# A gated attention and mixture-of-experts kernel: softmax denominators by on-chip transfers, reciprocals at step 11, and a reordered SyncE queue

## The reference, cut to what matters

```python
x = x + tanh(g_xattn) * cross_attention(layernorm(x), ctx)     # 8 heads, 512 queries, 512 keys
x = x + tanh(g_ffn) * moe(layernorm(x))                        # 8 experts, the best 2, and a shared one
# inside cross_attention, per batch and head
attn = softmax(q @ k.T / sqrt(16));  out = attn @ v
```

## Time and profile before

| what | value |
|---|---|
| runs, median (lowest to highest) | 1438.15 us (1435.48 to 1442.34) |
| the profiled execution | 1441.5 us, its span 1439.6 us |
| mean granted TensorE clock | 0.974 of full speed |
| TensorE, VectorE, ScalarE, GpSimd busy | 93%, 68%, 61%, 60% of the span |

### The profile page before, as it was taken

One profiled execution on the slowest core, in us unless ns is written; L12 is line 12 of the kernel. 1 busy time (PEld: TensorE's weight loads), 2 busy tenths in 40 slices (PEclk: granted clock), 3 DMA queues, 4 the chain that ended last, 5 costly groups with the idle time before them and its releaser, 6 DMA issues.

```text
span 1439.6 us, 24599 instructions
## 1 busy us (share of the span) xinstructions
PE 1339.7 (93%) x7290; PEld 648.5 (45%) x7290; DVE 974.5 (68%) x1661; ACT 872.5 (61%) x1720; POOL 867.6 (60%) x1278
## 2 busy tenths in 40 slices
PE   2899999999999989998989999989999999999997
PEld 1222222222222222232222222267778888888886
DVE  5888788988788878897878888656654333333332
ACT  2588787877777767786767777734333433333332
POOL 7447667767776777677767864633212555555553
PEclk7799999999999999999999999999999999999999
DMA  6566666666767666766666766276653788785655
GB/s 177 160 190 206 191 202 198 195 199 185 188 178 181 197 183 174 187 199 181 180 182 185 188 160 172 92 206 138 150 183 82 188 215 205 182 198 110 111 110 81
DMA packets 161308, 247.90 MB, mean 172 GB/s; under 512 B 33605, under 2 KB 58828, under 8 KB 161182
## 3 DMA queue, kind: packets, MB, share of 16 engines
q1 hardware_dynamic: 142926, 208.96, 51.6%
q0 software_dynamic: 18256, 37.38, 14.0%
HBM read 141.85 MB, written 103.88 MB: 171 GB/s over the span
## 4 chain that ended last, share of the span: by engine, by line
PE 34%; DMA 21%; SPq 12%; issue 11%; DVE 9%; POOL 8%; ACT 4%; POOLq 1%; ACTq 0%; DVEq 0%
PE m_banks L949 17%; DMA parts_k<-arena 11%; SPq L470 8%; DMA arena<-pv_d 6%; DVE row_max L1122 6%; PE bank L906 4%; PE bank L877 4%; PE m_banks L856 3%; PE bank L837 3%; SPq L456 3%; POOL xs L780 2%; DMA out<-xs,ids 2%; POOL arena L679 2%; POOL arena L676 2%; POOL arena L677 2%
## 5 line engine op out<-in xcount | busy, mean ns | idle before, releaser
L1122 DVE TENSOR_REDUCE row_max<-m_banks 128x2 f32<-128x1024 f32 x512 | 614.4, 1220 | 82.1 <-PE m_banks L856 77.5
L1394 ACT ACTIVATE arena<-bank 128x512 f32<-128x512 f32 x1024 | 556.6, 606 | 127.8 <-PE bank L877 124.8
L877 PE MATMUL bank<-arena 112*128 112x512 bf16 x1024 | 317.7, 389 | 6.0 <-ACT arena L1394 1.8
L906 PE MATMUL bank<-arena 128*32 128x512 f32 x2048 | 278.9, 617 | 0.3 <-ACT arena L1401 0.3
L792 POOL DMA_INDIRECT out<-xs,ids x71 | 112.5, 1584 | 173.6 <-ACT xs L1468 138.4
L856 PE MATMUL m_banks<-arena 48*128 48x512 bf16 x1024 | 169.7, 395 | 27.0 <-DVE row_max L1122 20.7
L877 PEld LDWEIGHTS bank<-arena 112*128 112x128 bf16 x1024 | 79.7, 100 | 255.5 <-ACT arena L1394 91.6
L949 PE MATMUL m_banks<-w_ring,h_hi 128*128 x568 | 183.1, 403 | 0.0
L1457 ACT ACTIVATE arena<-m_banks 128x256 f32<-128x256 f32 x103 | 39.5, 384 | 190.4 <-PE m_banks L949 190.3
L676 POOL TENSOR_TENSOR arena<-arena 128x512 bf16<-128x512 f32 x62 | 71.6, 1156 | 110.3 <-ACT arena L1386 107.4
L856 PEld LDWEIGHTS m_banks<-arena 48*128 48x128 bf16 x1024 | 39.7, 94 | 164.1 <-issue 81.9
(11 more groups left out here) (176 smaller groups left out, 2037.9 us busy)
## 6 DMA issues: line engine op xcount, KB each, us to landing
pv_d<-arena SPq DMA_DIRECT2D x32, 512.0 KB, 4.3
w_ring<-split_d SPq DMA_DIRECT2D x60, 256.0 KB
parts_k<-arena SPq DMA_DIRECT2D x96, 128.0 KB
parts_q<-arena SPq DMA_DIRECT2D x96, 128.0 KB
arena<-parts_k SPq DMA_DIRECT2D x64, 192.0 KB, 3.7
arena<-parts_q SPq DMA_DIRECT2D x64, 192.0 KB, 3.8
arena<-in_w SPq DMA_DIRECT2D x36, 256.0 KB, 7.0
arena<-in_ctx SPq DMA_DIRECT2D x32, 256.0 KB, 3.4
```

Source lines behind the costliest of these rows:

```text
L877: nc.tensor.matmul(out, k_stack[b % 3][0:SHIFTED, h, kt * P:(kt + 1) * P], q_stack[b % 3][0:SHIFTED, h, :], start=True, stop=True).then_in ...
L906: last = nc.tensor.matmul(pv_ps[2 * DH * j:2 * DH * (j + 1), :], v_ones[b % 3][:, kt, GROUP * g + j, :], probs[pair % 3][:, j, :], start=( ...
L1122: nc.vector.reduce_max(pair, m_ps[(STEPS * b + u) // 2 % M_PAIRS], AX_X).then_inc(s_mx, 1)
L1394: nc.scalar.activation(probs[group % 3][:, j, :], bank_of["scores", b, s], ACT.Exp, scale=float(DH) ** -0.5).then_inc(s_exp, 1)
```

## The change

Instead of reading the denominators back from memory, SyncE copies them inside SBUF, with one transfer per half g: 4 partitions of 512 words become 64 partitions of 32. It needs only that `take_values` has written both halves. These two transfers stand ahead of `store_values`. The reciprocals are taken at step 11 instead of 16. `store_reciprocals` moves ahead of `load_ctx` and `store_turned`. The next batch's row of maxima, `row(i + 1, 0)`, moves ahead of the query reads `read(i + 2, 1)`. `load_values` now waits for the landing of `store_values` itself, and `take_values` waits for the previous batch's on-chip transfers.

```diff
-RECIP_AT = 16
+RECIP_AT = 11
-            def load_denominators(b):
-                sp.wait_ge(s_w, DMA * (b + 1))
+            def spread_denominators(b):
+                sp.wait_ge(s_u, 2 * b + 2)
                 if b:
                     sp.wait_ge(s_rc, b)
-                sp.dma_start(den_c, pv_d[:, DH, :].rearrange("h (c w) -> h c w", c=DH)).then_inc(s_sc, DMA)
+                for g in range(2):
+                    sp.dma_start(den_c[P // 2 * g:P // 2 * (g + 1), :], pv_sb[DH:P:2 * DH, g, :]).then_inc(s_sc, DMA)
...
             def load_values(b):
                 sp.wait_ge(s_r, DMA * (b + 1))
+                sp.wait_ge(s_w, DMA * (b + 1))
...
                 if is_b(i - 1):
+                    spread_denominators(i - 1)
                     store_values(i - 1)
...
                 if is_b(i - 1):
-                    load_denominators(i - 1)
+                    store_reciprocals(i - 1)
                 if is_b(i + 4) and i + 4 >= 2:
                     load_ctx(i + 4)
                 if is_b(i - 3):
                     store_turned(i - 3)
-                if is_b(i - 1):
-                    store_reciprocals(i - 1)
+                if is_b(i + 1):
+                    row(i + 1, 0)
                 if is_b(i + 2):
                     read(i + 2, 1)
-                if is_b(i + 1):
-                    row(i + 1, 0)
...
                 if j == 0:
+                    spread_denominators(B - 1)
                     store_values(B - 1)
                 if j == 1:
                     store_turned(B - 3)
-                    load_denominators(B - 1)
...
             def invert(b):
-                dve.wait_ge(s_sc, DMA * (b + 1))
+                dve.wait_ge(s_sc, 2 * DMA * (b + 1))
...
                 if b:
                     act_e.wait_ge(s_w, DMA * b)
+                    act_e.wait_ge(s_sc, 2 * DMA * b)
                 nc.scalar.copy(pv_sb[:, g, :], pv_ps).then_inc(s_u, 1)
```

## The result

The changed kernel takes 1420.87 us in the median of 17 runs (1412.53 to 1432.76), against 1441.42 us for the kernel before, measured beside it (17 runs, 1435.48 to 1450.13). The ratio is 0.9856 [0.9833, 0.988]: 20.6 us gained, where 39.7 were forecast. The profiled execution took 1418.35 us, with a span of 1416.5.

What follows compares the result with a forecast made beforehand. The reciprocal's wait for denominators, queued on SyncE behind the reads of k, was taken as the bound. 42 - 4 + 1.7 = 39.7 us gained gave 1399 us against the median; range 1390 to 1411, chance 0.78.

Steps and rivals of the forecast that it cites:

- The 42 us: Reciprocal's wait at step 16 goes, each of 28 turns falling from 28.02 to 26.5 us; 42 gained, bounds nothing to 47.
- the wait that comes at step 11: Reciprocals moved to step 11 wait for late on-chip transfers; 4 us lost, range 1 to 29.
- The landings: On-chip transfers at step 11, measured by `row`: 2.8 us median, 6.0 worst; backlog 0.8 us later costs 6.7, 2 us 29.
- The price of a wait: At step 11: the first 0.9 us free in a turn, each us beyond costs about 1.2.
- Rival A: Wait moves from step 16 to 11, transfers landing 2 us or more later; 29 us lost, 1411 to 1425, chance 0.15.
- Rival B: Query reads behind the row come late, TensorE waits each turn; 81 us against 42 gained, 1477, chance 0.03.
- cost 0, 1.7 us to spare: Row of maxima ahead of query reads: last read landed at 22.6, wanted at 24.3 in a 26.5 us turn; cost 0.
- The last batch: End of the attention: `source(2)` goes out about 4 us earlier without the wait for the store; 1.7 us gained.
- The signs named in advance: Profile after: reciprocal's wait under 12 us, TensorE idle near 20, turns of 26.5 throughout, SyncE longest at row of maxima.

Runs made afterwards that it cites:

- number 1: The kernel after with the reciprocals back at step 16 instead of 11: 1401.81 us, 0.9742.
- number 2: The kernel after with the query reads ahead of the row of maxima again, reciprocals still at step 11: 1411.65 us, 0.9795.
- 3  on-chip, old order: The kernel before with the on-chip transfers alone: reciprocals at step 16, old order of store_reciprocals and query reads: 1411.62 us, 0.9799.
- 4  row first alone: The kernel before with only the row of maxima moved ahead of the query reads, denominators still read back from memory: 1493.21 us, 1.0366.
- number 5: The kernel after with load_values ahead of the row of maxima, reciprocals at step 11: 1434.84 us, 0.9959.
- 6  step 13: The kernel after with the reciprocals at step 13 instead of 11: 1409.78 us, 0.9789.
- 8  on-chip ahead of row: The kernel after with the two on-chip transfers ahead of row(i, 1) instead of behind it: 1417.56 us, 0.9842.
- 9  reads first, step 13: The kernel after with the query reads ahead of the row of maxima and the reciprocals at step 13: 1411.81 us, 0.9815.
- number 12: The kernel after with the two on-chip transfers issued by ScalarE on a queue of their own instead of by SyncE: 1425.77 us, 0.9891.
- 7: The kernel after with load_values ahead of the row of maxima and the reciprocals at step 13: 1435.17 us, 0.9945.
- number 10: The kernel before with the reciprocals at step 19 instead of 16, denominators still through memory: 1441.25 us, 1.0015.

## Why the prediction was half right

Read turn by turn (turns 2 to 29; the reciprocal's wait in all; when the slower `row` has landed, counted from the mark, in the mean):

```
kernel                     turn us   TensorE idle   wait   row landed   time
before                       28.01           49.0   53.0         6.02   1441.4
after                        27.21           32.5   16.9         6.94   1420.9
1  step 16                   26.65           25.3    0           7.35   1401.8
2  reads first               27.04           30.6    7.3         6.02   1411.7
3  on-chip, old order        26.93           29.0    0           6.98   1411.6
4  row first alone           29.92           82.5   79.8         7.09   1493.2
5  load_values early         27.46           44.0    1.0         4.41   1434.8
6  step 13                   26.92           26.5    3.9         7.17   1409.8
8  on-chip ahead of row      27.11           28.8   13.1         7.28   1417.6
9  reads first, step 13      26.95           29.4    2.1         7.08   1411.8
12 issued by ScalarE         27.68           40.4   14.3         7.51   1425.8
```

**The 42 us were nearly right.** VectorE's wait at the reciprocal did bound the kernel, and turns of 26.5 us were there to be had. Number 1 has 26.65 us a turn: 38 us over the 28 turns and 40 by the medians.

**The step that failed is the wait that comes at step 11**, taken at 4 us. It cost 19: number 1 differs from the kernel after by that step alone. The working had two factors, and both were low.
- *The landings.* They came 0.9 us later in the mean, and in the eight longest waits the reciprocal started some 0.4 us behind the slower `row`. I had worked out 6.7 us for 0.8 later and chose 4, for three quick turns that built up no backlog. (Counted again from the landings before, 0.8 us gives 6.3, and 2 us gives 23 and not the 29 that the prediction has.) The likely cause stood in the prediction's own account of the change: `load_values` issued later against the next turn. Number 2 takes much of that back and the landings are at 6.02 us again; number 5 puts it early and they are at 4.41.
- *The price of a wait.* The prediction had 0.9 us free in each turn and 1.2 us for each us beyond. The 16 turns of the kernel after in which the reciprocal waited 0.1 us or less last 26.54 us in the mean. The four with 0.2 to 1.0 us last 26.57, so a little waiting was free, as said. But the eight with 1.1 to 2.7 us (13.7 in all) last 28.88, together 18.7 us over. The rule would give 1.2 x (13.7 - 8 x 0.9) = 7.8. Half of the 18.7 is idle time of TensorE (2.04 us a turn for 0.83, 9.7 in all), and 2.0 us of that is for late query reads, in one turn. The other half is matmuls that take longer (26.84 us a turn for 25.71, 9.0 in all): five of the six half-clock stretches lie in four of these eight turns.

So even with the right landings I would have said 8 us, and the price is the larger error. It was fitted on waits at step 16 of the kernel before and carried over to step 11. Why a wait costs more there stays open. The query reads behind the row are not the reason, or not alone: in number 2 they stand in front of it, TensorE waits for none, and its three turns with waits of 1.1 to 1.9 us last 28.88 us in the mean too, each with a half-clock stretch.

**Rival A** names what happened: the wait moved to step 11. It priced it at 29 us, a tail at nothing, with half as likelier; the result, 1421, lies in its interval, 1411 to 1425, and its chance of 0.15 was too low. That the number fits is partly luck: the landings were not 2 us later, and the price of a wait was not the one it used. The argument against it, that the new transfers need only free rings, is what number 12 refutes: a ring of their own didn't help.

**Rival B** was there in small: 5.0 us of waits for query reads, at three places. Two of them, 3.1 us, lie in turns in which the reciprocal did not wait and the row went out as early as forecast (13.9 us after the mark at 838.92):

```profile
852.81 1.22 SPq L531 DMA_DIRECT2D arena<-m_rows  x2
854.08 3.88 SPq L470 DMA_DIRECT2D arena<-parts_q  x6
...
864.33 0.61 PE L857 MATMUL m_banks<-arena 48*128 48x512 bf16 x4 [2.15 <-DMA arena<-parts_q]
```

The last of the six was issued at 857.36 and reached TensorE 7.0 us later. The prediction allowed 3.9, from one turn of the kernel before, and named 5.6 as the limit. So "cost 0, 1.7 us to spare" was wrong by its landing time, and number 1, whose reciprocal never waits, has 4.6 us of the same waits. Numbers 4, 5 and 7 show it large.

**The last batch** was taken at 1.7 us and brought nothing. The read went out sooner, but TensorE's wait hung on the read before it, which SyncE issues ahead of the denominators.

**The signs named in advance**: SyncE does wait longest at the row of maxima (109.2 us), and the wait at the turned maxima is gone. The reciprocal's wait is 16.9 us, not under 12, idle time 32.5 us over 28 turns, not 20, and turns of 26.5 us stand in between longer ones. Waits of over 1 us were the sign of rival A; they came in 8 turns of 28, not in most.

**Left open**: why the slower `row` has landed 4.7 us after the mark in one turn of the kernel after (838.9) and 9.0 in another (130.2), with the same transfers around it; the chain in number 10; and why a wait at step 11 costs more than one at step 16.

## What to carry to other kernels

A consumer moved earlier should stand behind the worst landing that its producer has after the change, not behind the mean of before: step 16, 5 us later in the turn, cost nothing, and step 11 gave back half the gain. Don't carry the price of a wait from one place in a loop to another, and count the slower clock after a gap: here it was half of the price. And an edit to a queue has no price of its own: the same swap cost 51 us on the kernel before and 9 with step 11 behind the on-chip transfers, and with step 16 it was part of an edit that gained 10.

## What was not expected of the hardware

- A gap of 1 to 2 us on TensorE was followed by 3.4 us at 1.2 GHz in some turns, in which L907 took 1.94 us for 1.07. Between the kernel after and number 1, with 6 such stretches and 1, busy time makes more of the difference (8.7 us) than idle time (7.2).
- Transfers of a few KB landed 1.7 us after issue at best and 6.6 at worst, and a second queue for them changed that little.
- 512 KB issued ahead of six query reads cost TensorE 25.0 us in 18 waits for them, and brought the slower `row` of the next turn 2.5 us earlier (6.94 to 4.41 us after the mark).
